# Feed-forward layers of a decoder block by seven block products instead of eight, over pairs of token chunks

## The reference

```python
def conn_dense(kernel, x):
    w = jnp.where(kernel, jnp.asarray(1.0, x.dtype), jnp.asarray(-1.0, x.dtype))
    return x @ w
...
h = s0 * conn_dense(k0, x)
h = jax.nn.relu(h) * 2.0
h = ei_dense(h, k1, s1, P)
h = jax.nn.relu(h) * 2.0
return ei_dense(h, k2, s2, P)
```

## Time and profile before

| what | value |
|---|---|
| median of three runs | 2008.92 us (2007.97 to 2009.19) |
| the profiled execution, its own time | 2008.8 us |
| its span in the trace | 2007.0 us |
| granted TensorE clock, mean | 1.000 |
| PE busy | 1996.8 us, 99% |
| DVE, ACT, POOL busy | 65%, 48%, 41% |

### The profile page before, as it was taken

The page is one execution under the profiler, slowest core; times in us unless marked ns, Lnnn a source line. Parts: engine busy times, 40 slices in busy tenths (PEclk is TensorE's granted clock), DMA queues, the critical chain, the costliest instruction groups (busy, mean ns, idle before and its releaser), DMA issues.

```text
span 2007.0 us, 31687 instructions
## 1 busy us (share of the span) xinstructions
PE 1996.8 (99%) x10448; PEld 1690.1 (84%) x10448; DVE 1313.6 (65%) x2297; ACT 955.3 (48%) x2367; POOL 817.0 (41%) x709
## 2 busy tenths in 40 slices
PE   9999999999999999999999999999999999999999
PEld 7888888888888888888888888888887778888887
DVE  6867666676767676767777777777778763332422
ACT  5444545353536353535555555555556555232221
POOL 5444435352625253524555655556555420000000
PEclk9999999999999999999999999999999999999999
DMA  9838363636454554678646356363463671202011
GB/s 361 301 122 304 125 256 116 259 100 253 131 222 157 196 183 170 233 272 300 199 137 219 112 165 210 124 219 122 156 223 153 213 266 42 84 1 84 1 42 42
DMA packets 80740, 344.87 MB, mean 172 GB/s; under 512 B 8608, under 2 KB 9376, under 8 KB 66976
## 3 DMA queue, kind: packets, MB, share of 16 engines
q1 hardware_dynamic: 80672, 343.98, 48.9%
HBM read 208.15 MB, written 135.79 MB: 171 GB/s over the span
## 4 chain that ended last, share of the span: by engine, by line
PE 89%; DVE 2%; DMA 0%; ACT 0%; issue 0%; POOL 0%; DVEq 0%; SPq 0%
PE at_qbank L56 7%; PE at_qbank L55 7%; PE at_qbank L54 7%; PE at_out L54 6%; PE at_qbank L1366 6%; PE at_qbank L1365 6%; PE at_out L56 6%; PE at_out L55 6%; PE at_score L1055 6%; PE at_out L1102 5%; PE at_out L1106 5%; PE at_out L1103 5%; PE at_score L1046 3%; PE at_turned L1067 3%; PE at_value L55 1%; PE at_value L56 1%
## 5 line engine op out<-in xcount | busy, mean ns | idle before, releaser
L1539 ACT ACTIVATE at_probs<-at_probs,at_row_stats 128x128 f32<-128x128 f32 x512 | 198.6, 389 | 167.6 <-DVE at_row_stats L2206 167.6
L2249 DVE TENSOR_TENSOR at_acc<-at_out,at_acc 128x512 f32<-128x512 f32 x320 | 219.6, 690 | 58.7 <-PE at_out L1106 58.2
L1855 POOL TENSOR_TENSOR at_probs<-at_probs,at_row_stats 128x512 f32<-128x512 f32 x128 | 133.3, 1042 | 279.8 <-DVE at_row_stats L2211 279.8
L1545 ACT ACTIVATE at_pT_hi<-at_turned 128x512 fp32r<-128x512 f32 x128 | 76.5, 598 | 285.6 <-PE at_turned L1067 285.6
L54 PE MATMUL at_out<-at_wvo,at_val_hi 128*128 128x512 f32 x512 | 207.5, 405 | 1.8 <-DVE at_acc L2257 1.8
L1894 POOL TENSOR_TENSOR at_acc<-at_stage,at_acc 128x512 f32<-128x512 f32 x128 | 165.8, 1295 | 95.2 <-ACT at_stage L1515 89.7
L56 PE MATMUL at_out<-at_wvo,at_val_lo 128*128 128x512 f32 x512 | 200.2, 391 | 0.0
L55 PE MATMUL at_out<-at_wvo,at_val_hi 128*128 128x512 f32 x512 | 199.8, 390 | 0.0
L2257 DVE TENSOR_TENSOR at_acc<-at_out,at_acc 128x512 f32<-128x512 f32 x256 | 175.5, 686 | 30.2 <-PE at_out L56 28.1
L1102 PE MATMUL at_out<-at_wvo,at_val_hi 128*128 128x512 f32 x448 | 183.0, 409 | 2.2 <-POOL at_val_lo L1882 0.8
L1103 PE MATMUL at_out<-at_wvo,at_val_hi 128*128 128x512 f32 x448 | 175.1, 391 | 0.0
(11 more groups left out here) (262 smaller groups left out, 5175.1 us busy)
## 6 DMA issues: line engine op xcount, KB each, us to landing
parts_d<-at_rope_tmp SPq DMA_DIRECT2D x32, 1024.0 KB, 6.1
at_qrope<-parts_d SPq DMA_DIRECT2D x128, 256.0 KB, 5.3
wvo_d<-at_wvo SPq DMA_DIRECT2D x16, 2048.0 KB, 11.2
at_wvo<-wvo_d SPq DMA_DIRECT2D x16, 2048.0 KB, 8.2
ab_raw<-in_w_heads SPq DMA_DIRECT2D x32, 576.0 KB, 8.6
wvo_d<-at_wvo SPq DMA_DIRECT2D x16, 1024.0 KB, 6.9
at_wvo<-wvo_d SPq DMA_DIRECT2D x16, 1024.0 KB, 10.1
cr_ctx<-in_context SPq DMA_DIRECT2D x32, 512.0 KB, 6.4
```

The costliest lines, as they stand in the source:

```text
L1539: ins = act.activation(probs[i][:, j, :], probs[i][:, j, :], ACT.Exp, bias=nmax[i][:, j:j + 1], accum_out=sums[i][:, j:j + 1])
L1855: pool.tensor_tensor(probs[i][:], probs[i][:], rsum[i].unsqueeze(2).to_broadcast([P, PARTS, SEQ]), ALU.mult).then_inc(probs_ready, 1)
L2249: dve.tensor_tensor(at, outb[FACTORS[name][2]][:], at, ALU.add).then_inc(added, 1)
```

## The change

The feed-forward part is written anew. Two chunks go together (1024 tokens, `SUPERS` = 2), and each layer's product is cut into 2 x 2 blocks of 512 on both sides: inputs, signs and outputs. Seven block products (Winograd's form, named P1 to P7) take the place of eight. A block product is 4 output tiles x 4 input tiles x 2 passes = 32 matmuls of 512 columns. `L` counts the layers of both pairs of chunks from 0 to 5; L = 0, 1, 3, 4 are hidden layers and L = 2, 5 output layers. `FF_ORDER` is the order of the seven.

- The operands are blocks r11, r21, r12, r22 and four sums or differences of them, SUM1 to SUM4, which DVE makes (`feed_sums`, two instructions of 1024 columns each).
- Each operand is split again: ACT rounds the high half (`feed_high`), DVE makes the low half (`feed_low`), and for P5 and P7 POOL makes it (`FF_LOW_BY_POOL`). There are three buffers each for high half, low half and weights, so those of one product can be filled once the product three before is done.
- The sums of sign blocks are made in bytes, two at a time as 16-bit words (`sum_bits`, four DVE instructions a layer, the first time a layer is used). POOL turns a block into fp32 words for each product, 42 times (`feed_weights`), and flips some rows of layers 1 and 2 beforehand (`flip_inhibitory`).
- P6, P5 and P3 go on adding in the banks in which P1 stood (banks A), P7 and P4 in those of P2 (banks B). In hidden layers ACT copies what stands in banks A after P1, P6 and P5 into `kept` and `kept2` (`feed_keep`), DVE adds banks B to it after P2, P7 and P4 (`feed_add`), and ACT applies relu. In output layers DVE adds each bank into the rows (four instructions a product).
- Tiles 4 to 7 are normalised by ACT instead of DVE, and turned inside the first product. Tiles 8 to 15 are turned inside L = 2.

```diff
+    FF_ORDER = (("P1", "P2", "P6", "P5", "P3", "P7", "P4"), ("P1", "P6", "P2", "P5", "P3", "P7", "P4"),
+                ("P1", "P6", "P2", "P5", "P3", "P7", "P4"))
+    FF_ON_A, FF_OPENS, FF_KEPT = ("P1", "P6", "P5", "P3"), ("P1", "P2", "P7"), ("P1", "P6", "P5")
...
+    FF_LOW_BY_POOL = ("P5", "P7")
...
+        ff_w = [home(28672 + 8192 * i, f"ff_w{i}", [P, KH, CH], F32R) for i in range(3)]
...
+        ff_hi = [home(o, f"ff_hi{i}", [P, KH, CH], F32R) for i, o in enumerate((157696, 53248, 141312))]
+        ff_lo = [home(o, f"ff_lo{i}", [P, KH, CH], F32R) for i, o in enumerate((165888, 100352, 149504))]
+        r11, r21, r12, r22 = (home(o, f"ff_{n}", [P, KH, CH]) for n, o in (
+            ("r11", 174080), ("r21", 83968), ("r12", 124928), ("r22", 133120)))
...
+        banks_a = [qbank[0][:], qbank[1][:], down[1], value[:]]
+        banks_b = [outb[0][:], outb[1][:], turned[:], down[0]]
...
-            def feed_hidden(c, layer):
...
-                    for k in range(KT):
-                        if layer and m == 0:
-                            pe.wait_ge(hid_lo, HID * c + k + 1)
-                        wk = ff_w[layer][:, k, m * P:(m + 1) * P]
-                        pe.matmul(ff_lin[m % 2][:], wk, act_hi[of][k // 4][:, k % 4, :], start=k == 0, stop=False)
-                        ins = pe.matmul(ff_lin[m % 2][:], wk, act_lo[of][k // 4][:, k % 4, :],
-                                        start=False, stop=k == KT - 1)
-                    ins.then_inc(lin_ready, 1)
...
+                elif name in ("P7", "P4"):
+                    if name == "P7" and L == 2:
+                        pe.wait_ge(copied, 6 * BPC)
+                    pe.wait_ge(ff_summed, was_summed(L, {"P7": "P2", "P4": "P7"}[name], m))
+                else:
+                    before = {"P6": "P1", "P5": "P6", "P3": "P5"}[name]
+                    if l < 2:
+                        pe.wait_ge(kept_done, was_kept(L, before, m))
+                    else:
...
+            def block_product(L, name, behind):
+                g = at_product(L, name)
+                i = g % 3
+                pe.wait_ge(w_ready, g + 1)
+                for m in range(KH):
+                    bank_read(L, name, m)
...
+                        elif m == 0 and k % 2 == 0:
+                            pe.wait_ge(*made_low(L, name, k // 2))
+                        for x in (ff_hi[i], ff_lo[i]):
+                            last = k == KH - 1 and x is ff_lo[i]
+                            first = name in FF_OPENS and k == 0 and x is ff_hi[i]
+                            if L % LAYERS < 2:
+                                ins = pe.matmul(out, ff_w[i][:, k, cols], x[:, k, :], start=first, stop=last,
+                                                skip_group_check=True)
...
+            def feed_keep(L, name, m):
+                act.wait_ge(product_done, computed(L, name, m))
+                if name == "P5":
+                    act.wait_ge(relu_done, relu_11(L, m // 2))
...
+                to = kept2 if name == "P6" else kept
+                act.activation(to[:, m, :], banks_a[m], ACT.Copy).then_inc(kept_done, 1)
...
+            def feed_relus_11(L):
+                for z in range(2):
+                    act.wait_ge(ff_summed, was_summed(L, "P2", 2 * z + 1))
+                    act.wait_ge(*made_low(L, "P5", z))
+                    feed_relu(both(r11, z), both(kept, z), L, 2 * z)
...
-                    act.activation(hid[:, m % 2, :], ff_lin[m % 2][:], ACT.Relu,
-                                   scale=scale2[:, layer:layer + 1]).then_inc(relu_done, 1)
-                    act.wait_ge(relu_done, count + 1)
-                    act.activation(act_hi[to][m // 4][:, m % 4, :], hid[:, m % 2, :], ACT.Copy).then_inc(hid_hi, 1)
-                    if c == 0 and layer == 0:
-                        signs_to_weights(1 + m // 4, m % 4)
...
+                feed_high(L, "P5")
+                if l < 2:
+                    feed_keep_all(L, "P6")
+                    feed_high(L, "P3")
+                    feed_relus_11(L)
+                    feed_high(L, "P7")
+                    feed_keep_all(L, "P5")
+                    feed_high(L, "P4")
+                    feed_relus_12(L)
...
+            def feed_weights(L, name):
+                l, g = L % LAYERS, at_product(L, name)
+                block, less = FF_W[l // 2][name]
+                if g >= 3:
+                    pool.wait_ge(product_done, 4 * (g - 3) + 4)
+                if (L, name) == (0, "P6"):
+                    pool.wait_ge(bits_summed, 2)
+                elif L < LAYERS and name == ("P1" if L else "P5"):
+                    pool.wait_ge(bits_summed, 4 * (l + 1))
+                pool.tensor_scalar(ff_w[g % 3][:].rearrange("p k n -> p (k n)"), ff_bits[l][:, block, :], less, None,
+                                   ALU.subtract).then_inc(w_ready, 1)
+            def feed_low(L, name):
+                i = at_product(L, name) % 3
+                for z in range(2):
+                    pool.wait_ge(hi_done, made_high(L, name, z))
+                    pool.tensor_tensor(both(ff_lo[i], z), both(source(L, name), z), as_f32(both(ff_hi[i], z)),
+                                       ALU.subtract).then_inc(lo_by_pool, 1)
...
+                for L in range(LAYERS * SUPERS):
+                    for j, name in enumerate(FF_ORDER[L % LAYERS]):
+                        if at_product(L, name) >= 3:
+                            feed_weights(L, name)
+                        if name in FF_LOW_BY_POOL:
+                            feed_low(L, name)
+                        if L in (0, 1) and j == 2:
+                            flip_inhibitory(L + 1)
...
-            def feed_turn(c, t, half):
-                cols = slice(t * P, (t + 1) * P)
-                dve.wait_ge(ff_turn_hi, 2 * BPC * c + 2 * t + half + 1)
-                dve.tensor_tensor(act_lo[c % 2][half][:, :, cols], ff_turned[half][:].rearrange("p (k s) -> p k s", k=4),
-                                  as_f32(act_hi[c % 2][half][:, :, cols]), ALU.subtract).then_inc(ff_turn_lo, 1)
...
-                    dve.tensor_tensor(act_lo[to][m // 4][:, m % 4, :], hid[:, m % 2, :],
-                                      as_f32(act_hi[to][m // 4][:, m % 4, :]), ALU.subtract).then_inc(hid_lo, 1)
...
+            def feed_low(L, name):
+                i = at_product(L, name) % 3
+                for z in range(2):
+                    dve.wait_ge(hi_done, made_high(L, name, z))
+                    dve.tensor_tensor(part(L, name, ff_lo[i], z), part(L, name, source(L, name), z),
+                                      as_f32(part(L, name, ff_hi[i], z)), ALU.subtract).then_inc(lo_done, 1)
...
+                dve.scalar_tensor_tensor(out=u[to], in0=u[of], scalar=257.0 * plus, in1=u[other], op0=ALU.add,
+                                         op1=op).then_inc(bits_summed, 1)
...
+            def feed_add(L, name, m):
...
+                to = kept2 if name == "P4" else kept
+                dve.tensor_tensor(to[:, m, :], banks_b[m], to[:, m, :], ALU.add).then_inc(ff_summed, 1)
...
+            def feed_layer(L):
+                sc, l = L // LAYERS, L % LAYERS
+                if l == 0:
+                    feed_low(L, "P2")
+                    if L == 0:
+                        for j in range(4):
+                            sum_bits(0, j)
+                    feed_sums(L, SUM1)
+                    feed_sums(L, SUM2)
+                    feed_low(L, "P6")
+                else:
+                    feed_low(L, "P6")
+                    if l == 2:
+                        feed_adds(L, "P1")
+                    feed_low(L, "P2")
+                feed_sums(L, SUM4)
+                if l == 2:
+                    feed_adds(L, "P6")
+                feed_sums(L, SUM3)
+                if L < 2:
+                    sum_bits(L + 1, 0)
+                    sum_bits(L + 1, 1)
+                feed_adds(L, "P2")
+                if L < 2:
+                    sum_bits(L + 1, 2)
+                    sum_bits(L + 1, 3)
+                feed_low(L, "P3")
+                if L < 2:
+                    feed_moments(8 + 4 * L)
+                    feed_moments(9 + 4 * L)
+                if l == 2:
+                    feed_adds(L, "P5")
+                feed_low(L, "P4")
+                if L < 2:
+                    feed_moments(10 + 4 * L)
+                    feed_moments(11 + 4 * L)
+                    feed_variances(2 + L)
+                if l == 2:
+                    feed_adds(L, "P3")
+                if L + 1 < LAYERS * SUPERS:
```

724 lines of the change are left out of this document (484 added, 240 removed).

## The result

The changed kernel takes 2027.1 us (median of four runs, 2024.7 to 2029.4); the kernel before, beside it, 2009.1 (2008.0 to 2012.0). The ratio is 1.009, 95% interval 1.0076 to 1.0103: slower by 18 us, where 15 us faster was forecast, and outside the range. The profiled execution took 2027.1 us, its span is 2025.3.

A forecast was written before the change was run, and what follows sets the result against it. TensorE's matmuls were taken to bound the feed-forward part. From 2008.8 us, 43.6 saved and 28.8 added (waits, mostly at P3 from DVE and POOL excluding each other, plus opening and end) gave 1994, range 1970 to 2006.

The forecast's parts named there:

- the price of GpSimd's conversion: Weights' conversion of 2048 columns on POOL, not in the trace: between 1.83 and 2.09 us, taken as 1.9.
- the turn: How long one instruction excludes the other engine: conversion 1.8 us, POOL's low half 2.25, DVE's 1024 columns 1.05.
- The turns at one door: DVE and POOL exclude each other at SBUF by whole instructions; TensorE waits, chiefly ahead of P3, up to 10.5 us.
- L = 4 without a wait: Hidden layer with P2 third: P5's copy done at 28.2 us, before P3 is due at 29.1; wait 0.
- The saving: Feed-forward part: 192 of 1536 matmuls go, at 0.227 us each, 43.6 us.
- Rival 4: Distance between matmuls grows beside three busy engines; 0.02 us more would cost 27 and bring no change; chance 0.03.
- The clock: TensorE's clock falling to 1.2 GHz after long waits, 7.27 us more per product so run; not in the sum; 0.07.
- rival 2: Clock falls to 1.2 GHz, one product for each of the four longest waits: 29 us, 2023 in all; chance 0.07.
- The opening: Before the first product: longer low half delays the first matmul 0.5 us, extra DVE statistics in the cross-attention 0.3.
- Rival 1: Turns interleave better, DVE ahead at each tie; only the opening's waits and the end remain, 2.8 us: 1968; chance 0.20.
- the floor: Whole kernel with only the opening's waits and the end left beside the saved products: 1968 us.
- Rival 3: All bounds at once: POOL first at ties, conversions at 2.09 us, same clump in L = 4: 1997 to 2009; 0.10.

The follow-up runs named there:

- mul_add: Changed kernel with GpSimd's conversion written as times 1.0 plus a constant, still 2048 columns, in place of one subtraction: 2002.9 us.
- pool_idle: Changed kernel with all low halves on VectorE and all weight conversions after the first three left out, so products run on old weights: 1968.3 us.
- signs_later: Changed kernel with times-and-plus conversions in two halves, all low halves on VectorE, layers 0 and 1's byte sums behind P7's and P4's low halves: 1974.0 us.

## Why the prediction was wrong

**The step that failed** is the price of GpSimd's conversion, "twice the row at 1024 is 2.09 ... I take 1.9". The row of L1989 is of times 2.0, plus -1.0, and the new instruction is one subtraction. I took the like engine, tile and types for the like operation, and a form with less arithmetic for no dearer. It is 5.37 us alone and 5.73 in the median. The bounds of 1.83 to 2.09 were bounds of the length, not of the form; no row of the kernel before shows one operation alone on bytes, and that should have made the upper end open. With the price went the turn: I had a conversion block VectorE for 1.8 us, and this form blocks it for 3.45; VectorE's busy time is 1553.1 us with it and 1506.3 in mul_add, for the same work. The Trainium skill ("GPSIMD Engine Reference", Performance versus the Vector engine) has the cost per element set by the count of operations, and one and two alike; the runs differ, 5.37 us for one operation and 1.90 or 7.09 for two.

**With that term put right** (mul_add) 2002.9 us come out against 1994, and the rest can be checked step by step (us of gaps):

| place of the wait | predicted | mul_add | after |
|---|---|---|---|
| L = 0: P1; P6; P5; P3 | 1.35; 0.2; 0; 10.5 | 0.4; 3.4; 0; 5.9 | 0.4; 0.9; 4.1; 9.3 |
| L = 1, P3 | 6.4 | 5.7 | 3.7, and 2.6 at P5 |
| L = 2, transposes | 3.0 | 4.8 | 1.8, and 2.7 at P6 |
| L = 3, P3 | 2.1 | 2.3 | 5.0, and 2.2 elsewhere |
| L = 4 | 0 | 0 | 3.6 |
| L = 5, P3 | 4.0 | 7.0 | 3.5 |

The turns at one door, worked out from the earlier trace rows, gave 27.6 us of waits, and mul_add has 29.6. The mechanism holds: the prediction had all but 0.17 us of an instruction block the other engine, and for the quick form and the low halves it is all but 0.14 and 0.13. L = 4 without a wait held. That the totals agree to 2 us is luck in part, for single sizes were off in both directions: in L = 0 P6 had too little and P1 and P3 too much (10.5 against 5.9), and L = 5 too little (4.0 against 7.0). With the real price of the conversion, layer 0's waits spread to P5, and L = 4 has one. So of the 33.1 us by which I was wrong, 24.2 are the form (2027.1 less 2002.9), 6.5 of the rest are the lower clock and 2.0 the waits.

**The saving held**: 192 matmuls x 0.227 us, and outside the gaps and the lower level the distance is 0.227 still (1198 of the changed kernel's are 0.225 to 0.235 us). Rival 4 is out.

**The clock** was a rival with 0.07, and is a part of every run in which TensorE waits long: 12.3 us after, 6.5 in mul_add, nothing in pool_idle and in signs_later, whose longest gap is 2.0 us. It belonged in the sum: waits of 5 us and more were predicted, and the trace before held no row against a fall. It doesn't cost a whole product each time, as rival 2 had it: the 12.3 us are 62 matmuls, under two products in all. That the result lies near its 2023 is chance: gaps and opening are 47.4 us of what was lost.

**The opening** was given 0.5 + 0.3 and took 7.6 with the slow conversions, 0.8 in mul_add. So the forecast held for the quick form; that VectorE's normalisation can be shut out as well I had not seen, and it cost little as long as the conversion was short.

**Rival 1** gave 1968 if the turns interleave better, so that only the opening's waits remain. They don't in the changed kernel (39.8 us of gaps) nor in mul_add (29.6). pool_idle reaches the same time in another way, by taking nearly all of GpSimd's turns out: it confirms the floor, not the rival. The nearest to it with all the work in place is 1973.7 to 1975.6. **Rival 3**, all bounds at once, had 1997 to 2009 and covers the time of mul_add, not that of the kernel as it is.
